# Attention tiles interleaved with the chunks around them on one Trainium2 core

## The reference

```python
x = x + 0.5 * ffn(ln(x))     # called f = 0 here
x = x + attention(ln(x))
x = x + 0.5 * ffn(ln(x))     # f = 1, the same weights
# ffn: silu(z @ sg) * (z @ su) @ sd with 2048 inner channels (shared), plus a routed part:
#   8 experts of 1024 inner channels, 2 per token, 640 slots each
# attention: q, k, v = split(z @ w_qkv); q, k = rmsnorm(q) * ln_w, rmsnorm(k) * ln_w
#   16 heads of 16 channels, causal softmax in groups of 64 tokens, then @ w_proj
```

## Time and profile before

| | us |
|---|---|
| median of 3 runs (lowest, highest) | 2354.44 (2353.31, 2367.79) |
| the profiled execution: its time | 2362.39 |
| the profiled execution: its span, first to last instruction | 2360.6 |
| TensorE busy, VectorE busy, ScalarE busy, GpSimd busy | 2253.5, 1401.8, 960.9, 441.5 |
| mean granted clock of TensorE, as a share of 2.4 GHz | 0.951 |

### The profile page before, as it was taken

One profiled execution on the slowest core, in us unless ns is written; L12 is line 12 of the kernel. 1 busy time (PEld: TensorE's weight loads), 2 busy tenths in 40 slices (PEclk: granted clock), 3 DMA queues, 4 the chain that ended last, 5 costly groups with the idle time before them and its releaser, 6 DMA issues.

```text
span 2360.6 us, 38651 instructions
## 1 busy us (share of the span) xinstructions
PE 2253.5 (95%) x14464; PEld 2093.0 (89%) x14464; DVE 1401.8 (59%) x3182; ACT 960.9 (41%) x1942; POOL 441.5 (19%) x424
## 2 busy tenths in 40 slices
PE   7999999999999998889988887999999999999999
PEld 6888899999988886788888886888899999988888
DVE  6666556666644335787777874766646666643333
ACT  3333344555433223555444542333345555532222
POOL 2323201121110001322222220433212112110000
PEclk9999999999999999887777876999999999999999
DMA  9312135554451011000000000232124444351110
GB/s 283 106 57 82 43 113 132 138 121 103 101 152 37 24 44 41 1 1 1 1 1 1 1 1 25 101 99 82 47 73 113 100 102 111 88 144 55 54 54 18
DMA packets 194489, 168.41 MB, mean 71 GB/s; under 512 B 16905, under 2 KB 175037, under 8 KB 194304
## 3 DMA queue, kind: packets, MB, share of 16 engines
q1 hardware_dynamic: 176640, 144.57, 20.3%
q0 software_dynamic: 17664, 21.38, 5.1%
HBM read 104.32 MB, written 68.07 MB: 73 GB/s over the span
## 4 chain that ended last, share of the span: by engine, by line
PE 88%; DVE 8%; issue 2%; ACT 1%; DMA 1%; SPq 0%; POOL 0%; DVEq 0%; ACTq 0%; POOLq 0%
PE gate_p L290 28%; PE quad L290 26%; PE quad L323 21%; PE misc L323 4%; PE quad L454 4%; PE misc L440 3%; DVE k_t L1037 1%; DVE y_s L992 1%; DVE smax L1015 1%; DVE s_s L964 1%; DVE vl L975 1%; PE misc L349 1%; PE misc L341 1%; DVE qke L1024 1%; PE misc L360 1%
## 5 line engine op out<-in xcount | busy, mean ns | idle before, releaser
L887 DVE TENSOR_TENSOR h_s<-quad,sg_s 128x512 f32<-128x512 f32 (+2 forms) x512 | 302.4, 591 | 566.0 <-PE quad L290 535.1
L290 PE MATMUL gate_p<-zh,w 128*128 128x512 f32 (+2 forms) x2048 | 634.3, 356 | 2.3 <-DVE zl L736 2.3
L290 PE MATMUL quad<-zh,w 128*128 128x512 f32 (+2 forms) x2048 | 621.3, 349 | 0.0
L323 PE MATMUL quad<-w,hh 128*128 128x256 f32 x2816 | 559.9, 281 | 1.6 <-DVE hl L893 1.6
L574 ACT CAST hh<-h_s 128x512 fp32r<-128x512 f32 (+2 forms) x512 | 276.6, 540 | 667.6 <-DVE h_s L887 659.2
L323 PEld LDWEIGHTS quad<-w,hh 128*128 128x128 f32 x2816 | 460.1, 189 | 13.3 <-DVE hl L893 3.1
L569 ACT ACTIVATE sg_s<-gate_p 128x512 f32<-128x512 f32 (+2 forms) x512 | 265.2, 518 | 387.7 <-PE gate_p L290 383.8
L893 DVE TENSOR_TENSOR hl<-h_s,hh 128x512 fp32r<-128x512 f32 (+2 forms) x512 | 303.1, 592 | 191.4 <-ACT hh L574 176.0
L290 PEld LDWEIGHTS quad<-zh,w 128*128 128x128 f32 x2048 | 375.2, 189 | 41.6
L290 PEld LDWEIGHTS gate_p<-zh,w 128*128 128x128 f32 x2048 | 376.8, 189 | 35.7 <-DVE zl L736 2.8
L323 PE MATMUL quad<-w,hl 128*128 128x256 f32 x1408 | 395.2, 281 | 0.0
(11 more groups left out here) (165 smaller groups left out, 2745.3 us busy)
## 6 DMA issues: line engine op xcount, KB each, us to landing
stage<-in_L_ffn_rg SPq DMA_DIRECT2D x128, 128.0 KB, 2.7
stage<-in_L_ffn_ru SPq DMA_DIRECT2D x128, 128.0 KB, 3.0
stage<-in_L_ffn_rd SPq DMA_DIRECT2D x128, 128.0 KB, 3.1
slots_d<-empty SPq DMA_DIRECT2D x16, 662.5 KB, 7.7
zh_d<-zh SPq DMA_DIRECT2D x16, 512.0 KB, 3.2
zl_d<-zl SPq DMA_DIRECT2D x16, 512.0 KB, 4.5
y_d<-x SPq DMA_DIRECT2D x16, 512.0 KB, 5.9
zh<-zh_d SPq DMA_DIRECT2D x16, 512.0 KB, 4.1
```

The costliest lines, as they stand in the source:

```text
L290: last = pe.matmul(dst, a, b, start=(k == 0), stop=(k == 3 * n - 1))
L323: last = pe.matmul(out[:, j // 2, o:o + C], a[:, par, cols], w[:, hi, :], start=(c == 0 and i == 0 and j % 2 == 0), stop=(c == NCH - 1 and ...
L887: v.tensor_tensor(h_s[:, par, 0:ncol], up_p[:, par, 0:ncol], sg_s[:, par, 0:ncol], ALU.mult).then_inc(sm["h_done"], 1)
```

## The change

The loop over attention tiles is dissolved into a loop of 40 "fused" steps. A fused step works on two chunks, and on one attention step where there is one. The 40 steps cover the 64 chunks of `s1` of f = 0 and the 16 chunks of the first two blocks of `s0` of f = 1. Tile t has its statistics in step t + 4, q, k, v in t + 5, keys and scores in t + 6, transposed probabilities and values in t + 7, and projection in t + 8. In these steps:

- gate and up have one bank each, always the same; attention's products all go to the two banks of `quad`, one after the other (before, they had `gate_p`, four banks of `quad`, and `misc`);
- the rest `hl` of a chunk is made on GpSimd, not VectorE;
- the scores are masked straight into `p_s`, which is also what Exp reads and writes (before: `s_s` and `p_s`);
- the preparation of blocks 0 and 1 (and the start of block 2) of f = 1 goes with fused steps, where block 0's stood alone before; pieces of the first expert's weights are split later in s0 (`PIECE_AT`);
- Silu and Exp follow each other in every step on ScalarE;
- attention's weights are loaded and split at the start of `s1` (steps 0 to 2), GpSimd sets its constants in step 2;
- `azn`, `azh`, `azl` have one buffer, not two; `vh` and `vl` three, not four. `zh`, `zl`, `sg_s`, `h_s`, `hh`, `hl`, `zn` no longer share memory with attention.

The core of the diff (the loops over chunks outside the fused steps keep their order):

```diff
+        FSTEPS = (NB + BEHIND) * NCH // 2
+        LAG = {"stats": 4, "z": 5, "keys": 6, "probs": 7, "out": 8}
+        def bank_of(n):
+            return 0 if in_fused(n) else n % 2
 # TensorE; z, keys, probs, out are the tiles of step s; waits left out but for some
+            def fused_step(s):
+                pair_transposes(qcat, "a_qt")
+                y_transpose(out)
+                z_transpose(z)
+                gate(n, b % 2, c, buf, SB)
+                project(out)
+                pair_transposes(kcat, "a_kt")
+                qkv(z, out)
+                up(n, b % 2, c, buf, SB)
+                pair_transposes(p_s, "a_pt")
+                down_of(*chunk_before(f, phase, b, c))
+                scores(keys, z, out)      # waits a_qe, a_ke0, a_ke1, a_qn(z), a_vl(z), a_o(out)
+                gate(n + 1, b % 2, c + 1, buf, SB)
+                prep(pf, pb, c)
+                up(n + 1, b % 2, c + 1, buf, SB)
+                values(probs, keys, out)  # waits a_pl, a_vl, a_masked(keys), a_o(out)
+                down_of(f, phase, b, c)
+                prep(pf, pb, c + 1)
 # ScalarE
+                queries(keys, 0); copy(yh); copy(azh); queries(keys, 1)
+                silu(n, SB)
+                copy(k_t[0:64]); square q, square k (a_sq); values_high(z); copy(ph); twin(z)
+                h_high(n, SB); silu(n + 1, SB); prep(pf, pb, c); h_high(n + 1, SB)
+                Exp(p_s); prep(pf, pb, c + 1)
 # VectorE
+                yl; azl; x += projection; k_t[64:128]
+                extras(s - 1, 1)
+                qke; values_low(z); qk_normal(z)
+                h_product(n, SB)
+                pl
+                if c == 0: add_shared(previous block)
+                stats(ahead); masked(keys); h_product(n + 1, SB); subtracted(keys); normal(ahead)
+                extras(s, 0)
+                outputs(probs)
 # GpSimd
+                pow qkr(z)
+                prep_fused(s)             # ln, weight_exp, scatter of blocks 0 and 1
+                h_low(n)
+                pow ard(ahead); low parts qcat, kcat (z); subtract maximum (keys)
+                h_low(n + 1)
+            def h_low(n):
+                pool.wait_ge(sm["hh_done"], n + 1)
+                g.tensor_tensor(hl[:, n % 2, :], h_s[:, n % 2, :], hh[:, n % 2, :], ALU.subtract).then_inc(sm["hl_pool"], 1)
```

More of the change, by code:

```diff
@@ new lines, in pair_transposes, with scores @@
+            def pair_transposes(src, done):
+                for j in range(NH // 2):
+                    last = pe.transpose(misc[:, j // 4, (j % 4) * P:(j % 4 + 1) * P],
+                                        src[:, 2 * j:2 * j + 2, :].rearrange("p h d -> p (h d)"), ident[:, :])
+                last.then_inc(sm[done], 1)
+            def scores(t, z, out):
+                pe.wait_ge(sm["a_qe"], t + 1)
+                pe.wait_ge(sm["a_ke0"], t + 1)
+                pe.wait_ge(sm["a_ke1"], t + 1)
+                if z is not None:
+                    pe.wait_ge(sm["a_qn"], z + 1)
+                    pe.wait_ge(sm["a_vl"], z + 1)
+                if out is not None:
+                    pe.wait_ge(sm["a_o"], out + 1)
+                for j in range(NH // 2):
+                    o = (j % 4) * P
+                    for g in range(2):
+                        own = slice(GROUP * g, GROUP * g + GROUP)
+                        last = pe.matmul(quad[:, j // 4, o:o + P].rearrange("p (r c) -> p r c", r=2), q_t[:, j, g, :],
+                                         k_t[:, j, :, own], start=(g == 0), stop=(g == 1))
+                last.then_inc(sm["a_s"], 1)
@@ new lines, in values @@
+            def values(t, keys, out):
+                pe.wait_ge(sm["a_pl"], t + 1)
+                pe.wait_ge(sm["a_vl"], t + 1)
+                if keys is not None:
+                    pe.wait_ge(sm["a_masked"], keys + 1)
+                if out is not None:
+                    pe.wait_ge(sm["a_o"], out + 1)
+                q = t % VDEEP
+                for j in range(NH // 2):
+                    o = (j % 4) * 66
+                    last = split_product(quad[:, j // 4, o:o + 66], [(ph[:, j, :], pl[:, j, :], vh[:, q, j, :], vl[:, q, j, :])], 1)
+                last.then_inc(sm["a_y"], 1)
@@ L517, in _ @@
+            fused()
+            blocks(1, "s0", range(BEHIND, NB))
+            blocks(1, "e", range(NEB))
+            blocks(1, "s1", range(NB))
+            down_of(1, "s1", NB - 1, NCH - 1)
         @block.scalar
@@ new lines, in values_high @@
+            def values_high(t):
+                act.wait_ge(sm["a_v"], t + 1)
+                wait(act, sm["a_y"], t + 1 - VDEEP)
+                for g in range(2):
+                    for r in range(2):
+                        src = quad[64 * g:64 * g + 64, 1, 0:C].rearrange("p (j r d) -> p j r d", r=2, d=HD)[:, :, r, :]
+                        o = 32 * g + HD * r
+                        last = nc.scalar.copy(vh[64 * r:64 * r + 64, t % VDEEP, :, o:o + HD], src)
+                last.then_inc(sm["a_vh"], 1)
@@ L678, in _ @@
+            nc.scalar.copy(router[:, :, 0, :], router_s[:, :, :]).then_inc(sm["rt_in"], 1)
+            prep_high(0, 0)
+            for j in range(1, 4):
+                first_high(j)
+            blocks(0, "s0", range(NB))
+            blocks(0, "e", range(NEB))
+            fused()
+            blocks(1, "s0", range(BEHIND, NB))
+            blocks(1, "e", range(NEB))
+            blocks(1, "s1", range(NB))
         @block.vector
@@ L1147, in scatter @@
                     pool.wait_ge(sm["init"], 16 * NB * (f + 1))
-                for j in range(BT):
+                for j in tiles:
                     t = BT * k + j
@@ L1319, in _ @@
             for f in range(2):
-                save_z(f, 0)
+                if f == 0:
+                    save_z(f, 0)
                 shared_phase_0(f)
```

1088 lines of the change are left out of this document (561 added, 527 removed).

## The result

The changed kernel takes 2221.63 us (median of 4 runs, 2217.13 to 2225.82) beside 2361.11 us (4 runs, 2353.31 to 2368.76) for the kernel before: a ratio of 0.9409, 95% interval 0.9364 to 0.9454. The forecast was 2210.0 us. The profiled execution took 2220.21 us.

A forecast was written before the change was run, and what follows sets the result against it. Before: ffn bound by TensorE's matmuls, attention by VectorE nearly filling a step plus half clock after stalls. Forecast: 1500 outside + 669 TensorE work + 10 stalls + 26 preparation + 5 start = 2210 us, own range 2190 to 2235.

The forecast's parts named there:

- VectorE nearly fills a step at full clock: Attention stage before the change: VectorE busy 11.5 us a tile, a tile taking 14.8 us on average.
- TensorE's work, 669 us: Changed stretch at full clock: 80 chunks 330.4, 32 tiles 329.6, preparing three blocks 8.7 us; a full step 18.6 us.
- Stalls of 0.5 us a step, 10 us: TensorE waits in 20 fused steps without preparation; bounds 0 and 1.5 us a step.
- The walk: One full fused step timed through all engines: slack 0.1 us before scores, 0.9 before values, 0.5 before outputs.
- hl on GpSimd "costs nothing": Fused steps: GpSimd makes hl in 1.5 us each, within its slack; without the cover 0.8 us a chunk.
- Preparation, 26 us: Fused steps preparing blocks: 1.5 us stall in 12 steps, 18, plus refilled pieces in 4 steps, 8; bounds 5 and 48.
- Outside, 1500.2 us: Time outside the changed stretch, taken as unchanged; variation between executions put most likely on the clock in attention.
- rival E: ScalarE in fused steps: a table switch costs 1 us of every step, 2242 us; chance 0.04.
- rival D: VectorE's small routing instructions: each part waits out one GpSimd instruction, 1.5 us, 36 us in all, 2246 us; chance 0.12.
- Rival A: Changed stretch: TensorE never waits but at the start, 2174 us; chance 0.12.
- B: Attention chains in fused steps run late everywhere, 3.3 us a tile step, 106 us, 2280 us in all; chance 0.14.
- C: TensorE's clock in fused steps falls as in attention before, mean 0.78, giving 2399 us; chance 0.04.

## Why the prediction was right, and where it wasn't

- **What bounds the kernel.** "VectorE nearly fills a step at full clock" is wrong, as the kernel before with k_t on ScalarE shows: VectorE's load went down and the time up. "Half clock after its stalls does the rest" holds, and is the larger part: 3.4 us a tile against 1.5 us of waits, by the estimate above. The forecast survived since it didn't rest on that sentence: it asked only whether TensorE would wait in a full step.
- **TensorE's work, 669 us, and steps of 18.6 us.** Right but for 0.3 us a step: 18.9 us measured, TensorE busy all 18.90 us of a plain step, clock 1.00. About 0.16 of the 0.3 is the covered wait for the scores; what makes the rest wasn't taken apart.
- **Stalls of 0.5 us a step, 10 us.** The number came out (9.9 in steps 8 to 24), in part by luck: the plain steps have no named wait, and their 0.28 us, the 0.5 of the added product and two dips of the clock, which the forecast had not, make it up.
- **The walk.** Its slacks are confirmed in order and nearly in size. Scores: 0.1 forecast, none measured (the covered wait of 0.16 us, and 0.69 us put there cost 0.76). Values and outputs: 0.9 and 0.5 forecast; 0.69 us put ahead of both cost 0.06 in a plain step and 0.6 in one that adds the shared product. The 0.3 us that I gave that last step was 0.5.
- **hl on GpSimd "costs nothing".** Right in plain steps (1.33 us against my 1.5, and 18.9 us either way), wrong at the ends, where GpSimd's sums and scatters stand ahead: 5.6 us at the start, which the forecast had as its 5, and 3 to 4 us at the end, which it had not.
- **Preparation, 26 us.** Mis-sized: about 10, of it 7.4 us in named waits. I charged 1.5 us to each of 12 steps and the refilled pieces in full; most of that lay in slack. Against it stand 14.5 us where tiles come in and run out, which I had priced as pure TensorE work: 3.2 us are waits in steps 4 to 7 and 3.1 the wait in step 37, with half clock behind it. That few tiles in flight leave too little other work to lie over a chain is my reading; it wasn't tested. The two errors cancel by luck.
- **Outside, 1500.2 us.** 10.4 us too low in the profiled execution. Kernels with the same code there differ by 5 us at the start of the stretch, by waits and dips of the clock in single executions. The part behind the stretch was 827.1 to 828.2 us in the four profiles without a dip there and 829.2 to 831.4 in the eight with one or two (827.1 before). So I was wrong to put nearly all variation between executions into attention.
- **Rule on table loads (rival E).** The row decided rightly: of the 65 loads between Silu and Exp, 1.28 us each, each full step hides its two, and the next ACTIVATE starts 0.01 us after 64 of them. The rule's 32 us aren't there. The Trainium skill, "ScalarE: Activation LUTs", section "What ACT_TABLE_LOAD costs", is not borne out in its further 1.38 us.
- **Rule on the shared port (rival D).** My weighing was wrong: GpSimd's constant 1.548 us in rows 7 was the exclusion itself, with GpSimd always second. Alone it takes 1.04. The Trainium skill, "SBUF — State Buffer", section "SBUF: two separate sides", says that two such instructions exclude each other, and the traces agree. Its price was small here all the same: of VectorE's small preparation instructions in the stretch, 7 were held up, by 0.8 to 1.1 us each, 6.4 us in all, where D had 36 us.
- **Rival A** fell: TensorE waited 3.2 us in steps 4 to 7, 7.4 us in the steps with preparation and 3.1 us in step 37. **B** fell since, the start aside, only steps with preparation or few tiles waited for 0.8 us or more, **C** since the mean clock stayed at 0.99. The experiments with one more wait in each step (0.7 us for the scores) show that even then plain steps kept their full clock.

## What to carry to other kernels

When a stage has low clock and short TensorE waits, don't ask which engine is busiest there, but which wait each step ends on: relieving VectorE, which seemed nearly full, made this stage slower, and laying dense matmul work over it made the waits vanish in full steps. Walk one step through all engines and write down the slack of every wait; the walk told rightly where 0.7 us of VectorE's time was nearly free in a plain step and where it cost all of itself. Where a two-input VectorE instruction and a GpSimd one must meet and GpSimd has slack, let VectorE start first. And look at both ends of a pipeline, where queues of another stage still stand ahead.

## What the runs showed of the hardware

- VectorE with two SBUF inputs and GpSimd's two-input instructions exclude each other. Started within 0.05 us of each other, VectorE first, VectorE takes its 0.69 us and GpSimd 1.55 in place of 1.04; started 0.07 us later, VectorE waited out three GpSimd instructions in a row (4.01 us). A one-input `tensor_scalar` is held up too: the normed tile takes 0.40 us and up to 1.38, ending 0.15 us behind GpSimd's, where the maximum over 128x1024 was never held up (1219 to 1221 ns, 32 times).
- TensorE's clock dipped to half for some 3.4 us at two places where its records have no pause of over 0.15 us, behind runs of matmuls with 8 to 66 columns, at a cost of 1.3 and 2 us. Most runs of the same kind pass without a dip; what sets one off stayed open. Other dips stand behind waits, as in steps 0 and 37.
- In the kernel before, the wait for k_t longer by 0.5 us in each tile, and all waits together by 0.3, lowered the mean clock of the stage from 0.78 to 0.70; in plain interleaved steps a wait of 0.7 us in each cost only itself. What between the two makes the difference wasn't taken apart.
